# Front of a fused layernorm, attention and MoE kernel: ScalarE alternates normalising with high parts, two tiles are turned into other banks, one statistics step moves behind the low parts

## The reference, cut to what matters

```python
xn = layernorm(x)                     # x: 4 x 1024 x 1024, tokens x features, no gain
q, v, g = xn @ Wq, xn @ Wv, silu(xn @ Wg)
states[t] = sigmoid(beta) * states[t-1] + v[t]
attn = ((layernorm(q * states) * ln_g + ln_b) * g) @ Wo
logits = xn @ router_w.T              # 64 experts, the best 8 per token
ffn = sum over experts of w_e * (silu(xn @ w1_e.T) * (xn @ v1_e.T)) @ w2_e
out = x + attn + ffn
```

## Time and profile before

| | |
|---|---|
| median of 3 runs | 2477.35 us (2476.07 to 2477.9) |
| profiled execution | 2477.67 us |
| its span | 2476.0 us |
| PE busy | 2421.0 us (98%) |
| DVE busy | 1625.2 us (66%) |
| ACT busy | 1307.5 us (53%) |
| POOL busy | 675.8 us (27%) |
| mean granted TensorE clock | 0.994 |

### The profile page before, as it was taken

The page is one execution under the profiler, slowest core; times in us unless marked ns, Lnnn a source line. Parts: engine busy times, 40 slices in busy tenths (PEclk is TensorE's granted clock), DMA queues, the critical chain, the costliest instruction groups (busy, mean ns, idle before and its releaser), DMA issues.

```text
span 2476.0 us, 35288 instructions
## 1 busy us (share of the span) xinstructions
PE 2421.0 (98%) x12113; PEld 2098.4 (85%) x12113; DVE 1625.2 (66%) x1689; ACT 1307.5 (53%) x1435; POOL 675.8 (27%) x523
## 2 busy tenths in 40 slices
PE   7999999999999999999999999999999999999997
PEld 6888778888888888888888888888888888888886
DVE  7776798766666665666566666657666666656653
ACT  5557323654556654566445565455655456544653
POOL 3221122223323232322223222332233222323321
PEclk9999999999999999999999999999999999999998
DMA  7796855797668966779676797766986679867685
GB/s 276 262 315 198 254 188 200 252 300 235 197 222 277 309 222 215 234 252 298 239 234 211 256 308 248 236 217 224 316 273 197 227 234 292 271 216 234 221 273 158
DMA packets 143621, 606.10 MB, mean 245 GB/s; under 512 B 20592, under 2 KB 20656, under 8 KB 143024
## 3 DMA queue, kind: packets, MB, share of 16 engines
q1 hardware_dynamic: 116304, 518.91, 59.0%
q0 software_dynamic: 27232, 86.00, 16.2%
HBM read 520.89 MB, written 100.70 MB: 251 GB/s over the span
## 4 chain that ended last, share of the span: by engine, by line
PE 81%; DVE 9%; DMA 4%; ACT 4%; issue 2%; SPq 0%; POOL 0%; ACTq 0%; DVEq 0%; POOLq 0%
PE psA L1564 16%; PE psA L1565 16%; PE psA L1566 16%; PE psH L1564 5%; PE psH L1566 5%; PE psH L1565 5%; PE psY L1564 3%; PE psY L1566 3%; PE psY L1565 3%; DVE ew_lo L1169 3%; ACT ew_hi L770 3%; DMA ew_raw<-ew_dram 2%; PE psX L1677 2%; PE psY L1596 2%; DVE pw_lo L1164 1%
## 5 line engine op out<-in xcount | busy, mean ns | idle before, releaser
L1169 DVE TENSOR_TENSOR ew_lo<-ew_raw,ew_hi 128x1536 fp32r<-128x1536 f32 x384 | 694.0, 1816 | 331.4 <-ACT ew_hi L770 324.1
L770 ACT ACTIVATE ew_hi<-ew_raw 128x1536 fp32r<-128x1536 f32 x384 | 568.3, 1483 | 138.4 <-DMA ew_raw<-ew_dram 72.2
L1564 PE MATMUL psA<-xT_hi,pw_hi 128*128 128x512 f32 (+1 forms) x1544 | 612.1, 396 | 10.2 <-DVE pw_lo L1164 4.0
L1565 PE MATMUL psA<-xT_lo,pw_hi 128*128 128x512 f32 (+1 forms) x1544 | 603.7, 391 | 0.0
L1566 PE MATMUL psA<-xT_hi,pw_lo 128*128 128x512 f32 (+1 forms) x1544 | 603.5, 391 | 0.0
L764 ACT ACTIVATE pw_hi<-pw_raw 128x1024 fp32r<-128x1024 f32 x254 | 266.5, 1058 | 615.7 <-PE psA L1566 585.2
L1164 DVE TENSOR_TENSOR pw_lo<-pw_raw,pw_hi 128x1024 fp32r<-128x1024 f32 x256 | 317.5, 1247 | 128.9 <-ACT pw_hi L764 123.4
L1564 PEld LDWEIGHTS psA<-xT_hi,pw_hi 128*128 128x128 f32 x1544 | 292.2, 189 | 69.6 <-issue 13.2
L1564 PE MATMUL psH<-ew_hi,gT_hi 128*128 128x384 f32 x1024 | 346.4, 338 | 4.2 <-DVE ew_lo L1169 4.2
L1566 PEld LDWEIGHTS psA<-xT_hi,pw_lo 128*128 128x128 f32 x1544 | 291.9, 189 | 62.0
L1566 PE MATMUL psH<-ew_hi,gT_lo 128*128 128x384 f32 x1024 | 343.6, 336 | 0.0
(11 more groups left out here) (168 smaller groups left out, 3154.7 us busy)
## 6 DMA issues: line engine op xcount, KB each, us to landing
ew_raw<-ew_dram SPq DMA_DIRECT2D x384, 768.0 KB, 6.3
pw_raw<-proj_w_dram SPq DMA_DIRECT2D x256, 512.0 KB, 5.0
xn_scratch<-xt SPq DMA_DIRECT2D x33, 512.0 KB, 4.8
xt<-x_dram SPq DMA_DIRECT2D x32, 512.0 KB, 5.9
out_dram<-x_dram SPq DMA_DIRECT2D x32, 512.0 KB, 5.8
out_dram<-ot POOLq DMA_DIRECT2D x32, 512.0 KB, 8.9
xn<-xn_turned SPq DMA_DIRECT2D x29, 512.0 KB, 4.3
xn_turned<-xraw SPq DMA_DIRECT2D x28, 512.0 KB, 5.3
```

What stands on the lines that cost most here:

```text
L770: act.activation(ew_hi[:, c % 3, :], ew_raw[:, c % 3, :], ACT.Copy).then_inc(s_ewhi, 1)
L1169: dve.tensor_tensor(ew_lo[:, c % 3, :], ew_raw[:, c % 3, :], ew_hi[:, c % 3, :].bitcast(F32), ALU.subtract).then_inc(s_ewlo, 1)
L1564: pe.matmul(dst, l_hi, r_hi_, start=first, stop=False)
L1565: pe.matmul(dst, l_hi, r_lo_, start=False, stop=False)
```

## The change

Five things are different.

1. `bank_of`: tile 2 is turned into psY (before psA) and tile 3 into psX (before psY). psX also held tile 0.
2. ACT: before, it normalised tiles 0 to 3 and then made four high parts. Now it normalises tiles 0 and 1, and then takes turns: high part of 0, normalise 2, high part of 1, normalise 3, high parts of 2 and 3.
3. DVE: the statistics of tile 4 stood before the first `proj_lo` and the four `low`. Now `low(0)`, `proj_lo`, `low(1)` to `low(3)` come first, and the statistics of tile 4 stand behind them, directly ahead of those of tile 5.
4. PE, `turn_tile`: tile 3 waits until psX is free (`low(0)`, `s_plo` of 1), and tile 4, also in psX, waits for all four `low`.
5. PE, first projection: half c = 0 waits for `s_plo` of 2 (before 3), half c = 1 for 4 as before.

```diff
--- before.py
+++ after.py
@@ -330,7 +330,7 @@
 
         def bank_of(k):
 
-            return psA if k == 2 else psY if k == 3 else psX if k % 2 == 0 or k >= NTILE - KC else psH
+            return psY if k == 2 else psX if k == 3 or k % 2 == 0 or k >= NTILE - KC else psH
 
         LISTED = 2 * (SLOTS // 8) - 1
         ROUNDS_OUT = (0, 1, 1, 2)
@@ -836,10 +836,10 @@
 
             normalize(0)
             normalize(1)
-            normalize(2)
-            normalize(3)
             for k in range(NT):
                 turned_hi(k)
+                if k + 2 < NT:
+                    normalize(k + 2)
             act.wait_ge(s_rw, 16)
             act.activation(r_hl[:, :, 0:SEL], r_raw[:, :, :], ACT.Copy).then_inc(s_rhi, 1)
             act.wait_ge(s_par, 16 * N_PAR)
@@ -1291,10 +1291,11 @@
             for b in range(NB):
                 o = dve.memset(keep[:, b:b + 1], float(b % 2))
             o.then_inc(s_vconst, 1)
+            low(0)
+            proj_lo(0, 0)
+            for k in range(1, NT):
+                low(k)
             stats_tile(4)
-            proj_lo(0, 0)
-            for k in range(NT):
-                low(k)
             stats_tile(5)
             stats_of(2)
             proj_lo(1, 1)
@@ -1570,7 +1571,11 @@
             def turn_tile(k):
 
                 pe.wait_ge(s_xn, k + 1)
-                if k >= NTILE - KC:
+                if k == NT - 1:
+                    pe.wait_ge(s_plo, 1)
+                elif k == NT:
+                    pe.wait_ge(s_plo, NT)
+                elif k >= NTILE - KC:
                     pe.wait_ge(s_phi, k)
                     pe.wait_ge(s_plo, k - 1)
                 elif k >= NT:
@@ -1736,7 +1741,7 @@
                 turn_tile(k)
             pe.wait_ge(s_pwlo, 1)
             for c in range(2):
-                pe.wait_ge(s_plo, 3 + c)
+                pe.wait_ge(s_plo, 2 + 2 * c)
                 cols = slice(c * 2 * P, (c + 1) * 2 * P)
                 for k in range(KC):
                     if c == 1 and k == 0:
```

## The result

| | before | changed |
|---|---|---|
| median | 2478.18 us (20 runs, 2472.06 to 2483.55) | 2483.77 us (20 runs, 2476.66 to 2491.12) |
| span of the profiled execution | 2476.0 us | 2479.7 us |

The ratio is 1.0021, 95% interval 1.0014 to 1.0029: the changed kernel is 5.2 us slower (0.0021 x 2478), 3.5 to 7.2 by the interval. The forecast was 1.7 us slower (2479.0), and 2483.77 lies above its range, which ended at 2481.8.

A forecast was written before the change was run, and what follows sets the result against it. PE, busy for 98% of the span, was taken to bound the kernel. Profiled 2477.67 plus 0 for tile 4's turn, 1.7 for the slow stretch and 0 for the rest gave 2479.4, as a median 2479.0 us; range 2475.2 to 2481.8.

The forecast's parts named there:

- The mechanism: Front: first projection 1.5 us earlier, last low part not earlier, 3.0 us pause before tile 4's turn, clock falling behind it.
- nothing is lost further on: Behind tile 4's turn: VectorE work 1.2 us later was costed at nothing, at most 1.2 if its cover were gone.
- the price of the fall: Behind PE's new pause before tile 4's turn: the clock falls, costing 1.7 us out of bounds 0 to 1.7; 45%.
- start of turn 4, 26.6 - 26.59 = 0: PE's turn of tile 4 starts when it did in the profiled execution before, so the front gains 0.
- The slack of 1.2 us: Before the change, the chain through statistics, shift and normalising of tile 4 had only 1.2 us to spare against PE.
- The clock is already low when tiles 2 and 3 are turned: Rival, front: low clock at those turns, tile 4's turn at 27.5, +0.9, with the second fall +2.6, 2480.0; 20%.
- three short pauses: PE pausing three times between 14 and 17 us, where before it worked until 15.74.
- No fall: Rival, pause before tile 4's turn: the clock does not fall behind it, time 2477.4; 20%.
- POOL escapes the low part: Rival, front: POOL's power takes 0.69 instead of 1.60, tile 4's turn at 25.7, time 2476.5; faster within the front 8%.
- The rival on the other side: Slower by more than 0.2%: clock also falls at later pauses (56 to 66, 136 to 140), +6.0, 2483.4; 5%.
- The prediction's own evidence, the turns at the start: With nothing but transposes since 10.43, eight went from 1.94 to 1.04 us, against transposes not counting for the clock.

The follow-up runs named there:

- the fillings: Changed kernel with unread matmuls in PE's pause before tile 4's turn: 24 of 256 columns, ratio 1.0002; 26 of 128 columns, ratio 0.9998.
- tile 8 filled: Changed kernel with 20 unread matmuls of 256 columns ahead of tile 8's turn: 2479.21 us, ratio 1.0006 to the kernel before.
- Late logits: Changed kernel with the logits of tiles 0 and 1 moved behind the second projection: 2483.98 us, ratio 1.0022; again 2481.16, ratio 1.0020.
- doubled logits: Changed kernel with the logits of tiles 0 and 1 computed twice in a row: 2486.72 us (7 runs), ratio 1.0022.

## Why the prediction was wrong

**The mechanism was right.** Each step of the front stands where the working put it: projection 1.5 to 1.8 us earlier, last low part unmoved (18.77, before 19.04), shift at 24.72 (forecast 25.0), tile 4 at 26.21 (26.6), and a clock that falls behind the new pause. That nothing is lost further on was right as well (the fillings).

**The step that failed** is "The rows nearest in length are the 2.7 and the 3.53, both with a fall, so I take the fall and 1.7", the price of the fall. The term was mis-sized: 1.7 us assumed a stretch of 3.4 us, the length in the earlier trace rows. Measured in the changed kernel's four traces without filling, the slow time behind the pause is 10.2, 3.4, 13.7 and 13.7 us, that is 5.1, 1.7, 6.6 and 6.8 us of loss (0.5 us of the third stretch lay in the pause), 5.1 in the mean. I took the length of a slow stretch for a constant, because the stretches that I had read were 3.4. The same trace of before has a longer one near its end, with PE at work:

```profile
2455.00:2461.00 6.00, 5.69 (x13) 4.46 (x14) 0.26 (x1) 0.69 (x1) 0.18 (x1) 0.50 0.07 12
```

**A second step was right for one execution only:** "start of turn 4, 26.6 - 26.59 = 0". The 26.59 contains a slow stretch that the profiled execution had and others don't. With the clock up, the kernel before turns tile 4 at 24.72 or 25.02. Counted from the first turn that is 14.5 or 14.8, and the changed kernel's 15.85 is 1.0 to 1.3 us late. The slack of 1.2 us, which was to decide the case, was made by that slow stretch. In the first of the two traces ACT's normalising of tile 4 ends at 24.96, and PE, whose last matmul of the projection started at 24.70, takes up the turn at 25.02:

```profile
23.72 1.24 ACT L730 ACTIVATE xt<-xt,nmr,rs 128x1024 f32<-128x1024 f32 x1 [4.07 <-DVE nmr L1077]
```

I had subtracted a state of the clock as if it belonged to the kernel. Both errors point the same way.

**The rivals.** "The clock is already low when tiles 2 and 3 are turned" happened in two of five traces of the changed kernel, with turn 3 at 1.85 to 1.97 us and tile 4 at 27.0 to 27.3 (forecast 27.5); only one of the two fell again behind it. The prediction speaks there of three short pauses; the trace has two, 0.68 and 0.95. "No fall" happened once, in the execution with tile 8 filled, after a pause of 2.1 us. "POOL escapes the low part" didn't happen: the power took 1.60 again. The rival on the other side passed the 5 us, but not by its mechanism: not falls at later pauses, which both kernels have, but longer ones at the first.

**The clock, by the traces and by what is written of it.** The Trainium skill, TensorE: Matmul & The Clock Gate, says in Part 1 that how many matmuls run cold varies from run to run of one kernel, because the chip's watch over the activity is not tied to the kernel's start. The traces agree: the kernel before fell in the front, between 18 and 24 us, in two traces, and in two it didn't fall there at all. It should have kept me from pricing one trace's stretch. The rule in Part 4 of the same page of the Trainium skill, that transposes don't count as work for the clock, is not borne out: in the repetition of the changed kernel the stretch from 26.1 to 29.5 held 1.6 us of transposes and 1.9 us of logits, and the clock came back behind it. The prediction's own evidence, the turns at the start, rests on their durations alone: the rows of the granted clock read 1.00 from 10 us on, though eight transposes took 1.94 us there, as they do at 0.50 (1.97 in the trace of the changed kernel with the fall at 25.8).

**What stays open.** I found no rule for the length of a stretch. Late logits have a turn and then projections behind the pause, and a stretch of 3.4 us in all three traces; tile 8 has a turn, logits for some 3 us and then projections, and took 7 to 10 where it fell; the changed kernel's front, with the same kinds in the same order as tile 8, took anything from 3.4 to 13.7. Why late logits gain 2.5 us in M and next to nothing in the ratios isn't settled either, nor why doubled logits lose 9 us in M against the changed kernel (51.5 against 42.6), 3.5 of which were to be the added work, and next to nothing in the ratio. So M alone doesn't price a version whose logits have moved. With 11 or 12 runs, a ratio is known to 0.1%, 2.5 us.

## What to carry to other kernels

Before moving work out of a gap, ask which queue it will lengthen: here two statistics instructions that had filled VectorE's idle time became 1.2 us of the chain to the next tile, and undoing that one move gave the loss back within 0.1%. A pause of TensorE amid dense work has to be priced by the clock behind it, and by several traces, since one trace shows one state: the same pause of 2.0 to 2.8 us cost between nothing and 6.8. An earlier start pays only if the engine has ready work behind it; with the second projection there, the same change seems to be worth 2 to 3 us.

## What the runs showed of the hardware

- Stretches with a granted clock of 0.50 lasted 3.4, 6.8, 10.2, 13.7 and 20.5 us. A pause of 3.35 us went without one, and one of 1.98 us was followed by 13.7 us.
- Matmuls whose result nobody reads keep the clock up and can pay: 2.4 us of them in a pause of 2.35 us made the kernel before 0.17% faster (0.9974 to 0.9992). In a pause of 2.8 us, 26 of 128 columns (ratio 0.9998) did as well as 24 of 256 (1.0002).
